# A fused PixArt-style block in one kernel: first fc of the FFN ahead of the last MLP items, softmax scaling on GpSimd, joined halves

## What is computed

```python
x_in = _ln(ctx_n);  k = x_in @ wk + bk;  v = x_in @ wv + bv       # slots start from q_mu + exp(q_logsig) * layernorm(x)
for _ in range(3):
    prev = slots
    q = _ln(slots) @ wq + bq
    attn = softmax(k @ q.T / scale, axis=-1) + 1e-8
    attn = attn / attn.sum(axis=1)
    slots = (attn.T @ v) @ wu + bu + prev
    h = _ln(slots) @ w1 + b1
    slots = gelu(h) @ w2 + b2 + slots
    slots = _ln(slots + cond)
x = x + slots
h = gelu(layernorm(x) @ ternary(W_fc).T)          # 256 -> 1024
x = x + layernorm(h, ln_w, ln_b) @ ternary(W_proj).T
```

## Time and profile before

| | us |
|---|---|
| median of 3 runs | 339.01 |
| lowest, highest | 336.94, 339.3 |
| the profiled execution | 339.19 |
| its span (first to last instruction) | 337.3 |
| PE busy | 316.9 (94%) |
| DVE busy | 292.9 (87%) |
| ACT busy | 235.6 (70%) |
| POOL busy | 202.2 (60%) |

### The profile page before, as it was taken

How to read it: one execution, slowest core, us unless ns; L and a number is a source line. 1 busy time by engine, 2 the same in 40 slices (tenths; PEclk the granted TensorE clock), 3 DMA queues, 4 the chain that set the end, 5 groups by cost and what they waited for, 6 DMA issues and landing times. The chain is left out here.

```text
span 337.3 us, 6560 instructions
## 1 busy us (share of the span) xinstructions
PE 316.9 (94%) x1758; PEld 261.0 (77%) x1758; DVE 292.9 (87%) x851; ACT 235.6 (70%) x563; POOL 202.2 (60%) x385
## 2 busy tenths in 40 slices
PE   8899999999999989999998999799976899999994
PEld 8787888888887878888887788687853577767773
DVE  3699977899899889998999899999998789999874
ACT  2368986967467867785589674855638588898881
POOL 3168966255689764568987547377754944444341
PEclk9999999999999999999999999999999599999999
DMA  7988000000000000000000000000000000000001
GB/s 274 329 320 357 1 1 2 0 0 2 2 0 2 0 2 2 0 3 1 0 2 0 1 2 1 0 3 1 0 2 0 1 34 31 33 31 0 32 34 62
DMA packets 5311, 13.22 MB, mean 39 GB/s; under 512 B 672, under 2 KB 672, under 8 KB 4896
## 3 DMA queue, kind: packets, MB, share of 16 engines
q1 hardware_dynamic: 4160, 10.88, 8.6%
q10 hardware_dynamic: 1120, 1.98, 1.6%
HBM read 10.76 MB, written 2.10 MB: 38 GB/s over the span
## 5 line engine op out<-in xcount | busy, mean ns | idle before, releaser
L290 DVE BATCH_NORM_STATS2 stats<-S 128x6 f32<-128x256 f32 (+1 forms) x112 | 42.0, 416 | 9.3 <-DMA S<-ctx 3.5
L341 PE MATMUL ps_mid<-XT,KT 128*128 128x256 f32 x192 | 46.1, 383 | 3.4 <-ACT XT L357 3.4
L341 PE MATMUL ps_low<-V,PR 128*128 128x257 f32 x192 | 46.2, 383 | 1.7 <-DVE PR L863 1.7
L341 PE MATMUL ps_low<-wn,GT 128*128 128x256 f32 x192 | 45.7, 381 | 0.8 <-ACT GT L639 0.8
L341 PE MATMUL ps_mid<-XT,wt 128*128 128x256 f32 x192 | 45.5, 380 | 0.7 <-ACT XT L357 0.7
L341 PEld LDWEIGHTS ps_low<-V,PR 128*128 128x128 f32 x192 | 36.0, 190 | 8.4 <-DVE PR L863 3.5
L636 ACT ACTIVATE PR<-ps_mid,nmax 128x256 f32<-128x256 f32 x48 | 22.3, 471 | 27.3 <-DVE nmax L873 27.2
L341 PEld LDWEIGHTS ps_low<-wn,GT 128*128 128x128 f32 x192 | 36.1, 190 | 6.7 <-ACT GT L639 1.9
L341 PEld LDWEIGHTS ps_mid<-XT,KT 128*128 128x128 f32 x192 | 34.6, 190 | 8.4 <-ACT XT L357 4.6
L308 POOL TENSOR_TENSOR lnm_ab<-lnm_mv,mhalf 128x2 f32<-128x2 f32 x24 | 17.2, 715 | 38.9 <-DVE lnm_mv L298 38.9
L357 ACT ACTIVATE XT<-ps_t 128x512 f32<-128x512 f32 x56 | 33.1, 591 | 9.2 <-PE ps_t L333 9.2
(11 more groups left out here) (124 smaller groups left out, 706.4 us busy)
## 6 DMA issues: line engine op xcount, KB each, us to landing
S<-ctx SPq DMA_DIRECT2D x8, 256.0 KB, 3.8
X<-x SPq DMA_DIRECT2D x8, 256.0 KB, 3.4
out<-X SPq DMA_DIRECT2D x8, 256.0 KB, 2.0
rowv<-rows SPq DMA_DIRECT2D x1, 1920.0 KB, 9.9
wf<-w_fc_t SPq DMA_DIRECT2D x1, 1024.0 KB, 11.8
wf<-w_proj_t SPq DMA_DIRECT2D x1, 1024.0 KB, 13.8
wt<-w_tr ACTq DMA_DIRECT2D x1, 512.0 KB, 4.2
wn<-w_nat ACTq DMA_DIRECT2D x1, 512.0 KB, 5.8
```

The source lines that it names most:

```text
L290: dve.bn_stats(ln.st[:, at, j, 0:6], tiles[:, j]).then_inc(ln.stats_done, 1)
L341: last = pe.matmul(dst(m), lhs_t[:, c, m * P:(m + 1) * P], rhs[:, c, 0:n], start=(c == 0), stop=(c == 1))
```

## The change

- **Scaling.** The two `tensor_scalar` of `PR` an attention item move from VectorE to GpSimd, at the top of GpSimd's step.
- **Order on VectorE.** The row maximum comes before the statistics of Y.
- **X plus lnp_b** (`shift_x`). Before: items 0 to 7 in steps 7 to 10 of the last round, two items a step. After: items 0 to 4 one a step in the last five steps of round 1's loop, 5 and 6 in steps 7 and 8 of the last round, 7 in step 11.
- **Banks.** `fc` writes `ps_low[1 - rt]` (both banks), `hidden_t` writes `ps_mid`. In the last round the second MLP product goes to the two halves of `ps_low[0]`, so that `ps_low[1]` is free; the small products for the ln_b row move to `ps_low[1]`.
- **Joined.** gelu, square and the centred product are one instruction of 1024 elements each instead of two of 512; their sums need no addition.
- **Entry.** rows_t(0) moves ahead of the MLP product of step 15, low_parts(0) ahead of VectorE's item tail, fc(0) and gelu(0) to the end of step 15, centre(0) ahead of the tail of step 16, rows_t(1) and low_parts(1) into step 16, hidden_t(0), fc(1) and the rest of block 0 into step 17. ScalarE's copy_high(0) now stands before gelu(0), and gelu(0) before the gelu of MLP item 7.

```diff
+        def mlp_out(r, b):
+            return ps_low[0][:, b % 2] if r == ROUNDS - 1 else ps_low[b % 2][:, 0]
...
+                if it := item(t, s, 2, last):
+                    r, half, b = it
+                    if half == 0:
+                        pool.wait_ge(rinv_ready, r * B + (b + 1))
+                        pool.sem_inc(pool_held, 1)
+                        for j in range(J2):
+                            pool.tensor_scalar(PR[:, b % 4, j], PR[:, b % 4, j], rinv[:, b, j:j + 1], EPS_ATTN,
+                                               ALU.mult, ALU.add).then_inc(attn_ready, 1)
...
-                act.activation(Gf[:, rt, h * HALF:(h + 1) * HALF], ps_mid[h][:], ACT.Gelu,
-                               accum_out=gsum[:, rt, h:h + 1]).then_inc(gelu_done, 1)
+                act.activation(Gf[:, rt], ps_low[1 - rt][:].rearrange("p h n -> p (h n)"), ACT.Gelu,
+                               accum_out=gsum[:, rt:rt + 1]).then_inc(gelu_done, 1)
...
                 if s == STEPS - 1:
                     copy_high(0, 0)
-                if s in (FFN_STEP, FFN_STEP + 1):
-                    ffn(0, 0, s - FFN_STEP)
+                    gelu(0, 0)
+                if s == STEPS:
+                    square(0, 0)
+                    copy_high(1, 1)
+                if s == STEPS + 1:
+                    high_half(0, 0, 0)
+                    high_half(0, 0, 1)
+                    gelu(1, 1)
+                    square(1, 1)
...
-                for h in range(2):
-                    dve.scalar_tensor_tensor(out=GC[:, rt, h * HALF:(h + 1) * HALF],
-                                             in0=Gf[:, rt, h * HALF:(h + 1) * HALF], scalar=gneg[:, rt:rt + 1],
-                                             in1=rowv[:, ROW_LNW + h * HALF:ROW_LNW + (h + 1) * HALF],
-                                             op0=ALU.add, op1=ALU.mult).then_inc(gc_done, 1)
+                dve.scalar_tensor_tensor(out=GC[:, rt], in0=Gf[:, rt], scalar=gneg[:, rt:rt + 1],
+                                         in1=rowv[:, ROW_LNW:ROW_LNW + H],
+                                         op0=ALU.add, op1=ALU.mult).then_inc(gc_done, 1)
...
+            def before_tail(s):
+                if s == STEPS - 1:
+                    low_parts(0, 0)
+                if s == STEPS:
+                    centre(0, 0)
...
-                for b in range(2 * (s - LEAD), min(2 * (s - LEAD) + 2, B)):
-                    for j in range(J2):
-                        dve.tensor_tensor(X[:, b, j], X[:, b, j], row("lnp_b"), ALU.add).then_inc(x_shifted, 1)
+                if s in (LEAD, LEAD + 1):
+                    shift_x(s - LEAD + 5)
+                if s == LEAD + 4:
+                    shift_x(B - 1)
...
-                if s == STEPS - 1:
-                    low_parts(0, 0)
-                if s in (FFN_STEP, FFN_STEP + 1):
-                    ffn(0, 0, s - FFN_STEP)
+                if s == STEPS:
+                    low_parts(1, 1)
+                    stats_f(2, 0)
+                if s == STEPS + 1:
+                    low_half(0, 0, 0)
+                    low_half(0, 0, 1)
+                    centre(1, 1)
+                    apply_f(2, 0)
...
-                if it := item(t, s, 2, last):
-                    r, half, b = it
-                    if half == 0:
-                        dve.wait_ge(rinv_ready, r * B + (b + 1))
-                        for j in range(J2):
-                            dve.tensor_scalar(PR[:, b % 4, j], PR[:, b % 4, j], rinv[:, b, j:j + 1], EPS_ATTN,
-                                              ALU.mult, ALU.add).then_inc(attn_ready, 1)
...
+                if t == ROUNDS - 2 and s >= STEPS + 2 and not last:
+                    shift_x(s - STEPS - 2)
...
             def fc(b, u, r, rt):
                 if rt == 0:
                     pe.wait_ge(xtl_ready, b + 1)
+                if isinstance(r, int) and r == 0:
+                    pe.wait_ge(low_read, 2 * (T_FFN - B) + 2 * RING)
+                    pe.wait_ge(lnb_copied, 3)
+                elif isinstance(r, int) and r == 1:
+                    pe.wait_ge(low_read, 2 * T_FFN + 2 * RING)
+                else:
+                    pe.wait_ge(gelu_done, r - 1)
...
+            def hidden_t(r, rt):
+                pe.wait_ge(gc_done, r + 1)
                 for h in range(2):
                     if isinstance(r, int) and r == 0:
                         pe.wait_ge(mid_read, 2 * T_FFN + 2 * RING)
                     else:
-                        pe.wait_ge(gelu_done, 2 * r + (h - 1))
...
+                        pe.wait_ge(gtl_ready, 2 * r + (h - 1))
                     for k in range(4):
-                        last = pe.transpose(ps_low[rt][:, h, k * P:(k + 1) * P],
+                        last = pe.transpose(ps_mid[h][:, k * P:(k + 1) * P],
...
                 if s == STEPS - 1:
-                    rows_t(0, 0)
-                if s in (FFN_STEP, FFN_STEP + 1):
-                    ffn(0, 0, s - FFN_STEP)
+                    fc(0, 0, 0, 0)
+                if s == STEPS:
+                    rows_t(1, 1)
+                if s == STEPS + 1:
+                    hidden_t(0, 0)
+                    fc(0, 0, 1, 1)
...
+                if last and s == STEPS - 1:
+                    rows_t(0, 0)
                 for r, half, b in staged(t, s, LOW, last):
```

88 lines of the change are left out of this document (41 added, 47 removed).

## The result

| | before | after |
|---|---|---|
| median of the runs, us | 338.81 (20 runs) | 340.11 (20 runs) |
| lowest, highest | 336.94, 339.46 | 338.85, 343.12 |
| the profiled execution, and its span | 339.19, 337.3 | 338.88, 337.0 |
| PE, DVE, ACT, POOL busy | 316.9, 292.9, 235.6, 202.2 | 314.7, 271.1, 227.5, 222.2 |

The ratio of the changed kernel to the one before is 1.0061, with an interval of 1.0039 to 1.0084: slower by 0.6%, within the 1% that the forecast of 339.8 called no change.

What follows compares the result with a forecast made beforehand. TensorE was taken to bound the slot rounds, but not the FFN entry, where VectorE's sequence counts. Terms +2.7 - 2.2 - 0.6 + 0.5 = +0.4 gave 339.6, 339.4 as median, and 339.8 with 0.4 for instruction starts; range 335 to 344.5.

Steps and rivals of the forecast that it cites:

- The price: On GpSimd, one softmax scaling of 256 columns was taken to cost 0.50 us, between 0.3 and 0.75.
- Item 1: Rounds: scalings on GpSimd close a two-step loop, 0.22 us over TensorE's 7.80; queues behind b2 adds and at changes add more.
- The fold: Rounds 0 and 1, steps that fold ternary weights: the loop computed 0.93 us too long, taken as 0.7.
- The b2 queue: Round 0, step 2: the first scaling waits behind GpSimd's eight b2 additions, +1.5 us.
- Items 2 and 3: Rounds: earlier row maximum, -0.9 us at each of two changes; moved X additions, -2.8 for three waits, +1.8 for VectorE's load.
- Item 4: FFN entry: reordering and a free bank start fc(0) 4.3 us earlier, gaining 1.2 to 3.5 by the clock; -2.2 taken.
- Item 5: FFN row blocks: joined gelu, square and centring save 0.1 us a batch element, six of them, -0.6.
- Item 6: End of the kernel: with banks swapped, the last transposes wait and the last projections start later, +0.5 us.
- A: Rival: GpSimd's scaling costs only 0.4 us and the clock holds at the entry, 335.7 us; chance 0.22.
- B: Rival: GpSimd becomes the bound, with a scaling at 0.7 us, 344 us; chance 0.18.
- C: Rival: the FFN entry gives 0 instead of -2.2, fc(1) late and the clock down, 342 us; chance 0.13.
- D: Rival: scalings are hidden because VectorE, 0.6 us a step lighter, runs ahead; rounds +0.5, 337.5 us; chance 0.17.

Runs made afterwards that it cites:

- only_scaling_moved: The kernel before with one edit, the softmax scalings on GpSimd at the head of its step: 342.04 us, ratio 1.0114.
- before_busy: The kernel before with 21 more matmuls, results unread, where TensorE waits at the FFN entry: 336.66 us, ratio 0.9968.

## Why the prediction was right or wrong

The time was right (339.8 against 340.11) and so was "within 1%", but by terms that missed and cancelled, which is luck. At equal clock the forecast's terms are 2.7 for the rounds, 1.2 gained at the entry, 0.6 gained by the joins, 0.5 and 0.4 lost in the tail and at instruction starts: +1.8, where 2.6 was measured. For the clock it took 1.0 off (2.2 in place of 1.2), where the medians show 1.3.

- **The price** 0.50: right, 0.488. The estimate of the prediction from the Trainium skill ("GPSIMD Engine Reference", section 3.1) was about 0.42; the row decides.
- **Item 1, the loop**: right. It was read from the earlier trace rows as closing over two steps, with items 4 and 6 late, and they are. The plain excess of 0.22 measured 0.16 and 0.15 at item 4 of rounds 0 and 1; in round 2, where 0.2 was taken twice, 0.66 and 0.24. The fold was 0.7 and measured 1.22: 0.23 is my discount of the computed 0.93, and most of the other 0.29 the coefficients (1.36 for 1.10). Items 2 at the changes, taken as 0.4 late, waited 0.29 and 0.57. The b2 queue, 1.5, measured 1.65 on the first product and 2.2 when removed. In all, item 1 was 5.5 without the gains and measured 5.0 on top of the rest.
- **Items 2 and 3, what the waits belonged to**: wrong, and this is the step that failed. I booked the two waits of 0.35 on the order of the maximum and the three of 0.7 on the additions to X, 0.9 each. All went with the scaling alone. The two edits themselves, predicted at -1.8 and -1.0, measured +1.0 and +0.4 in their full context, and together -0.46 with the scaling on VectorE. What the rows show in their place is that GpSimd's additions stretched the scalings (0.62 to 1.36 and 1.51 a pair). My text had even noted that the additions made *the scalings* late, and then credited their move instead of the scalings' own.
- **The rounds**: +2.7 predicted, +4.3 measured (73.18 + 67.76 + 53.51 less 190.14). By rounds +2.4, +0.9, -0.6 became +3.4, +2.5, -1.6. Of round 1, 0.7 us is in no term: its last MLP products start 0.3 later by a longer wait for gelu (0.51 for 0.19), the change to attention waits 1.42 for 1.22, and one step between is 0.2 longer.
- **Item 4, the entry**: -2.2, with -1.2 and -3.5 for the clock falling again or not. Measured -3.9 with it up, and some -2 with it down (29.0 to 29.3 in two runs, against 31.13). At equal clock it is -1.2 (28.48 before, 27.24 after), the size forecast; the cause was not the order. Neither the order nor the joins alone account for the 1.2 (27.16 and 27.28 without them). The 28.48 holds the added matmuls; only_scaling_moved, less its fall at fc(0) (2.55 for 1.90), has 28.16, which would leave 0.9. Banks, or that either of the two would do, are left; that was not tried.
- **Item 5, the joins**: -0.6, measured -0.4 in the row blocks. **Item 6, the tail**: +0.5, measured +0.4, and 0.55 where the joins were undone.
- **The clock** was a term at the entry only. I did not see that a median of the kernel before contains 2.5 us of it, nor that the wait I predicted at 56.27 would open a second place. The loss at equal clock, 2.6, became 1.3 in the medians, because the kernel before lost to the clock in 50 of 64 executions and the changed one in 10 of 20.
- **Rivals**: A (cheap GpSimd) and B (p over 0.6) fell with p = 0.488. C (the entry gives nothing): fell, though the gain is not the order's. D (hidden anyway) fell for GpSimd. Its ground, VectorE ahead of where I had it, holds: with it, and with no scaling left to meet GpSimd's additions, the five waits went.

## What to carry to other kernels

When work moves to an in-order engine, price its place in the queue before its duration: put what other engines wait for directly behind its last input and optional work after it. Here the same GpSimd instructions gave 338.9 or 333.5 us at full clock. Several waits can share one cause and go with one edit, so no neighbour edit may book them too: of the five here only two named the scaling as what they waited for, the other three a copy on ScalarE. An instruction that takes far longer than its median in some places (1.51 for 0.62 a pair) points at the cause, and each edit run alone shows it. And compare kernels at equal granted clock, or by stretches, before an edit is praised or blamed.

## What the runs showed of the hardware that was not expected

TensorE's clock falls behind the same gap in some executions and not in others: behind 1.9 us of waiting, the same product took 2.00 in five profiles and 3.37 to 3.50 in three. Behind the gap of 2.4 to 2.6 us ahead of fc(1), fc(1) with fc(2) took 3.63 in four profiles and 5.31 in three. With two such gaps the executions of one kernel lie up to 4.3 us apart (338.85 to 343.12). From 2.4 GHz it goes to 1.2: 16 matmuls took 3.62 at the low level and 1.91 at the high one. Matmuls that compute nothing, put into the gaps, cost some 0.3 us at most (336.66 against 336.33, medians of before_busy and of the kernel before at full clock) and held it: all 24 executions of the three kernels with the entry covered so and no long wait in round 0 had a mean clock of 0.998 or more.

A GpSimd tensor_scalar of 256 columns with a scalar read from memory took 0.479 to 0.488 us, where after has 0.204 for one with two columns and 0.741 for an addition of two inputs of 256 columns. A VectorE tensor_scalar pair of 256 columns took 0.62 us by itself and 1.51 beside a pair of such additions on GpSimd.
